# Sorting attention scores from their SBUF copy, whole groups a group ahead, and half of a row sum moved to GpSimd

## The reference, cut to what matters

```
def sparsemax(z):                       # over the 32 patterns
    z_sorted = -sort(-z)
    cum = cumsum(z_sorted)
    support = 1 + k * z_sorted > cum    # k = 1..32
    k_sup = sum(support)
    tau = (cum[k_sup - 1] - 1) / k_sup
    return maximum(z - tau, 0)
...
scores = einsum('blhe,bshe->bhls', queries, keys)
A = sparsemax(scale * scores)
out = einsum('bhls,bshd->blhd', A, values) @ Wo + bo
x = x + layernorm(out)
```

## Time and profile before

| | us |
|---|---|
| median of 3 runs | 487.43 |
| lowest and highest run | 486.13, 487.61 |
| the profiled execution, its time | 487.64 |
| the profiled execution, its span | 485.9 |

### The profile page before, as it was taken

The page is one execution under the profiler, slowest core; times in us unless marked ns, Lnnn a source line. Parts: engine busy times, 40 slices in busy tenths (PEclk is TensorE's granted clock), DMA queues, the critical chain, the costliest instruction groups (busy, mean ns, idle before and its releaser), DMA issues. The chain is left out here.

```text
span 485.9 us, 6975 instructions
## 1 busy us (share of the span) xinstructions
PE 403.1 (83%) x2091; PEld 248.2 (51%) x2091; DVE 310.0 (64%) x1177; ACT 232.1 (48%) x424; POOL 151.9 (31%) x251
## 2 busy tenths in 40 slices
PE   3886566779888987997879999999998679999981
PEld 3542223235444554665646775634443237888870
DVE  3599999969999987586214236233332124979984
ACT  2226647747686795778444734100000001355765
POOL 3105645454858522432201110010000000344453
PEclk9997888788999998999998999999997879999997
DMA  4294011011010229367219667749999999601223
GB/s 145 88 300 127 8 44 43 1 43 38 8 43 2 76 88 309 117 217 275 103 56 316 246 215 262 261 181 395 395 391 396 392 377 368 221 1 45 86 88 129
DMA packets 44030, 83.78 MB, mean 172 GB/s; under 512 B 1878, under 2 KB 36316, under 8 KB 39388
## 3 DMA queue, kind: packets, MB, share of 16 engines
q1 hardware_dynamic: 42936, 82.15, 48.0%
q10 hardware_dynamic: 1060, 1.22, 0.8%
HBM read 70.78 MB, written 12.58 MB: 172 GB/s over the span
## 5 line engine op out<-in xcount | busy, mean ns | idle before, releaser
L1063 PE MATMUL bank<-Wz,yT 128*128 128x512 f32 x128 | 71.0, 707 | 25.9 <-DVE top L1640 23.2
L1063 PEld LDWEIGHTS bank<-Wz,yT 128*128 128x128 f32 x128 | 28.1, 228 | 61.6 <-issue 48.1
L1640 DVE MAX8 top<-bank 128x8 f32<-128x32 f32 x512 | 51.5, 181 | 1.9 <-ACT arena L736 1.7
L997 ACT ACTIVATE d<-d 128x32 f32<-128x32 f32 x16 | 3.7, 229 | 90.6 <-DVE d L2020 90.6
L576 POOL TENSOR_SCALAR veps<-mv 128x4 f32<-128x4 f32 x24 | 6.0, 248 | 107.0 <-DVE mv L1568 75.3
L684 POOL TENSOR_TENSOR work<-work 128x512 f32<-128x512 f32 x16 | 16.6, 1061 | 66.2 <-DVE work L2085 66.2
L1096 PE MATMUL bank<-aWo,hoT 128*128 128x256 f32 x128 | 36.0, 404 | 0.1
L715 ACT ACTIVATE arena<-arena,shift,rstd 128x256 f32<-128x256 f32 x64 | 33.2, 594 | 3.7 <-POOL shift L699 2.9
L1130 PE MATMUL bank<-arena,Wd 128*128 128x512 f32 x64 | 29.2, 598 | 3.2 <-ACT arena L799 3.2
L1159 PE MATMUL bank<-d,work 128*128 128x256 f32 x128 | 30.3, 382 | 0.9 <-ACT d L827 0.9
L1501 PE MATMUL bank<-scr,work 128*128 128x256 f32 x128 | 29.1, 381 | 1.6 <-ACT work L1010 1.6
(11 more groups left out here) (262 smaller groups left out, 879.0 us busy)
## 6 DMA issues: line engine op xcount, KB each, us to landing
arena<-in_L_ffn_e_W_dram SPq DMA_DIRECT2D x10, 1024.0 KB, 7.8
x<-in_L_ffn_e_W_dram SPq DMA_DIRECT2D x9, 1024.0 KB, 9.2
arena<-in_L_ffn_e_Wg_dram SPq DMA_DIRECT2D x7, 1024.0 KB, 11.2
scr<-in_L_ffn_e_W_dram SPq DMA_DIRECT2D x7, 1024.0 KB, 13.7
work<-in_L_ffn_e_W_dram SPq DMA_DIRECT2D x5, 1024.0 KB, 13.7
xin<-in_L_attn_query_dram SPq DMA_DIRECT2D x8, 512.0 KB, 4.1
x<-in_L_attn_query_dram SPq DMA_DIRECT2D x1, 4096.0 KB, 16.6
out_dram<-x SPq DMA_DIRECT2D x8, 512.0 KB, 5.6
```

Source lines behind the costliest of these rows:

```text
L1063: mm = pe.matmul(bZ[t % 2][:, :], yT[:, c, t * P:(t + 1) * P], Wz[:, c, :], start=(c == 0), stop=(c == C - 1))
L1640: mx = v.max(top[:, h * TG + t, :], bZ[t % 2][:, h * NS:(h + 1) * NS])
```

## The change

The sort reads the scores from their copy in SBUF instead of from the bank, so PE only waits until ScalarE has copied a tile (z_sb) and not until DVE has sorted it. In batch 0 the scores of a whole group are made together, a group ahead: PE runs turn_y and four tiles, ScalarE copies four tiles before the signs of the group. DVE sorts all four tiles of group i+1 ahead of the count of group i; threshold comes right behind settle. Group 5's last two tiles, which stood among the heads of batch 0, are made before them. In batch 0 GpSimd adds, behind the roots, the upper 16 of each row of clamped differences to the lower 16 (add_halves, into a free part of arena, semaphore added), and DVE's row sum runs over the 16 results. DVE's loop over groups 1 and 2 is written out. In batch 1 the order of DVE's work stays.

```diff
+        halved = arena[:, 12288:13312]
...
+            def add_halves(i):
+
+                hold(relued, i * 2 + 2)
+                rows_ = d[:, :].rearrange("p (r s) -> p r s", s=NS)
+                pool.tensor_tensor(halved.rearrange("p (r s) -> p r s", s=NS // 2), rows_[:, :, 0:NS // 2],
+                                   rows_[:, :, NS // 2:NS], ALU.add).then_inc(added, 1)
...
             with pool.Fori(0, GB - 1) as i:
                 subtract(i, 0)
                 roots(0, i + 2)
+                add_halves(i)
                 lower(i, 0)
             subtract(GB - 1, 0)
             roots(0, GB + 1)
+            add_halves(GB - 1)
             lower(GB - 1, 0)
...
-            put_scores(1, 0, range(2))
+            put_scores(1, 0, range(TG))
             with act.Fori(0, GB - 2) as i:
                 clamp(i)
                 mark(i)
                 norm_y(i + 2)
-                put_scores(i + 1, 0, range(2, TG))
                 put_yT(i + 2)
-                put_scores(i + 2, 0, range(2))
+                put_scores(i + 2, 0, range(TG))
                 signs(i, 0)
-            clamp(2)
...
+            for i in range(GB - 2, GB):
+                clamp(i)
+                mark(i)
+                norm_y(i + 2)
+                put_yT(i + 2)
+                put_scores(i + 2, 1, range(TG))
+                signs(i, 0)
...
             norm_y(6)
-            put_scores(5, 1, range(2, TG))
             put_yT(6)
...
                     if n >= 2:
-                        pe.wait_ge(topped, n - 1)
+                        pe.wait_ge(z_sb, n - 1)
...
-            scores_of(1, range(2))
+            scores_of(1, range(TG))
             for i in range(GB):
-                scores_of(i + 1, range(2, TG))
                 turn_y(i + 2)
-                scores_of(i + 2, range(2))
+                scores_of(i + 2, range(TG))
...
             heads_of(0, range(3))
-            scores_of(5, range(2, TG))
             turn_y(6)
...
-            def sort_top(i, tiles):
+            def sort_top(i, b, tiles):
 
                 for t in tiles:
                     hold(z_sb, i * TG + (t + 1))
                     for h in range(NH):
-                        mx = v.max(top[:, h * TG + t, :], bZ[t % 2][:, h * NS:(h + 1) * NS])
+                        mx = v.max(top[:, h * TG + t, :],
+                                   scr[b][:, h, bass.ds(i * TG + (t - b * KT), 1), :].rearrange("p o s -> p (o s)"))
                     mx.then_inc(topped, 1)
...
-                v.wait_ge(relued, i * 2 + 2)
-                v.tensor_reduce(exc[:, :], d3, AX_X, ALU.add).then_inc(newton, 1)
+                if b == 0:
+                    hold(added, i + 1)
+                    v.tensor_reduce(exc[:, :], halved.rearrange("p (r s) -> p r s", s=NS // 2), AX_X, ALU.add).then_inc(newton, 1)
+                else:
+                    v.wait_ge(relued, i * 2 + 2)
+                    v.tensor_reduce(exc[:, :], d3, AX_X, ALU.add).then_inc(newton, 1)
...
-            def batch_of_scores(i, b):
+            def batch_of_scores(i, b, nb=0):
 
                 first_statistics(i + 2)
-                sort_top(i + 1, range(2))
+                sort_top(i + 1, nb, range(TG))
                 count(i, b, True)
                 settle(i, b, True)
-                sort_top(i + 1, range(2, TG))
                 threshold(i + 1)
 
             batch_of_scores(0, 0)
-            with v.Fori(1, GB - 1) as i:
+            for i in range(1, GB - 1):
                 batch_of_scores(i, 0)
-            batch_of_scores(GB - 1, 0)
+            batch_of_scores(GB - 1, 0, 1)
```

More of the change, by code:

```diff
@@ L249, in build @@
         diff = sem("diff")
+        added = sem("added")
         relued = sem("relued")
@@ L1908, in _ @@
             own(split3(ab3[:, :], bo3))
-            sort_top(0, range(2))
+            sort_top(0, 0, range(2))
             fold_dispatch()
-            sort_top(0, range(2, TG))
+            sort_top(0, 0, range(2, TG))
             threshold(0)
             keep_dispatch()
-            def batch_of_scores(i, b):
+            def batch_of_scores(i, b, nb=0):
                 first_statistics(i + 2)
-                sort_top(i + 1, range(2))
+                sort_top(i + 1, nb, range(TG))
                 count(i, b, True)
                 settle(i, b, True)
-                sort_top(i + 1, range(2, TG))
                 threshold(i + 1)
             batch_of_scores(0, 0)
-            with v.Fori(1, GB - 1) as i:
+            for i in range(1, GB - 1):
                 batch_of_scores(i, 0)
-            batch_of_scores(GB - 1, 0)
+            batch_of_scores(GB - 1, 0, 1)
             check(0)
@@ L1935, in _ @@
                 v.wait_ge(cum, i * 3 + 3)
-                sort_top(i + 1, range(2))
+                sort_top(i + 1, 1, range(2))
                 if g > 0:
@@ L1942, in _ @@
                 settle(i, 1, False)
-                sort_top(i + 1, range(2, TG))
+                sort_top(i + 1, 1, range(2, TG))
                 threshold(i + 1)
```

## The result

| | before | after |
|---|---|---|
| median | 487.47 us (486.13 to 487.61, 4 runs) | 504.19 us (503.9 to 505.02, 4 runs) |
| ratio after/before | | 1.0349 [1.0327, 1.0371] |
| profiled execution, span | 487.64 us, 485.9 us | 504.1 us, 502.0 us |
| first check (flagi), end of batch 0 | 108.44 | 122.78 |
| second check, end of batch 1 | 190.04 | 203.83 |

The change costs 16.7 us, 3.5%. The forecast was 493.1 with a range up to 496: the sign is right and the size is wrong by 11 us. The profiled executions say where: 14.3 us are lost up to the first check, batch 1 gives back 0.5 (81.05 us from check to check, before 81.60), and 2.3 are lost behind it. The two spans differ by 16.1.

The account below looks back on a forecast made before the run. The prediction took DVE's queue to bound the front part. Longer batch 0 cycles, with DVE blocked by GpSimd's lowering, gave +6.65 us and the end of batch 0 -1.0: +5.65, forecast 493.1 us, range 487 to 496.

Parts of the forecast that it names:

- DVE's queue: Front part of the kernel, both batches: claimed to be as long as DVE's work, busy 66 of 69 us and 75 of 82.
- The end of batch 0: Last signs and flag of batch 0: flag's reduce 2.3 us after the last tau instead of 3.29, giving back 1.0 us.
- T: End of DVE's reduce that makes tau, from which cycles are counted; the last in batch 0 was forecast at 111.80.
- the forecast's better case for DVE: DVE's batch 0 cycle if the scan goes first and the multiply-add waits for GpSimd's lowering: 18.52 us.
- rival 4: Batch 0, later still: bursts stay at the low clock or the addition takes over 2.3 us; 496 to 498, chance 0.05.
- PE's slack: PE waiting for ScalarE's copy instead of the sort: PE is not the bound, so the edit was put at nothing.
- The addition: GpSimd's adding of halves behind the roots in batch 0: taken as 1.91 us, hidden by the sort with no room.
- Rival 1: Batch 0, nothing blocked: the scan passes beside GpSimd's lowering; cycle 16.1 us, -1.9 us, 485.5, chance 0.10.
- rival 2: Batch 0, scan and multiply-add both go ahead of GpSimd's lowering: cycle 17.8 us, +3.6 us, 491.0, chance 0.10.
- Rival 3: The sort, MAX8 cheaper from SBUF: 487 to 490.5, chance 0.08; by the page's full difference about 472, chance 0.02.
- The lock: Batch 0, scan or multiply-add blocked by GpSimd's lowering: cycles of 18.52 or 18.80 us; the blocked forecast had 0.65.
- the middle: Batch 0 cycle taken as 18.66 us, between 18.52 (scan first) and 18.80 (scan blocked).

Follow-up runs that it names:

- e6: After, with tiles made in pairs as in before and nine matmuls without use on PE ahead of the batch 0 transposes: 494.4 us, ratio 1.0143.
- e5: After, with PE running nine matmuls without use between the clamp and the transposes in batch 0: 498.22 us, ratio 1.022.
- e4: Before, with the sort reading SBUF, PE waiting for ScalarE's copy instead of the sort, and DVE's loop written out: 487.85 us, ratio 1.0022.
- e8: Before, with the sort reading SBUF and DVE's loop written out, but PE still waiting for the sort: 486.6 us, ratio 0.9984.
- e1: After, with the multiply-add's second factor read from a copy in PSUM in batch 0: 506.0 us, ratio 1.040.
- e7: After, with tiles in pairs, nine matmuls without use ahead of the transposes, and the multiply-add's factor in PSUM in batch 0: 492.31 us, ratio 1.0093.
- e3: After, with tiles made in pairs as in before and the multiply-add's factor in PSUM in batch 0: 497.41 us, ratio 1.0224.
- e12: Before, with the sort reading SBUF, PE waiting for the sort, and the scan's factors in PSUM in batch 0: 485.59 us, ratio 0.9987.
- e2: After, with before's order on PE and ScalarE, two tiles made ahead of the clamp and two ahead of the signs: 497.45 us, ratio 1.021.

## Why the prediction was wrong

**What bounds the kernel.** Right for before, wrong for after: "DVE's queue" became a round over ScalarE and PE, at 20.3 to 20.7 us for each group, where DVE and GpSimd would allow the 18.8 to 18.9 of e6 (forecast 18.66).

**The step that failed is "The end of batch 0", with the last sentence on steady cycles.** It counted "eight score matmuls", up to 6.59 us. The row with x8 in the earlier trace rows is two tiles: the kernel issues two matmuls for each tile, and the trace has four records for each. So four tiles are sixteen, 8.7 to 9.2 us in after. It also took PE's times from before, where the transposes run at the high level (1.22 us, granted clock 1.00); in after they are 1.98 at 0.50. By that wrong count the signs ended at the latest at T+20.9; in the first cycle of after they end at T+24.6, of which the burst is 2.6 us more than the 6.6 allowed for it and yT 0.8, and in the second at 81.21, T+26.4, well into the next cycle. "In steady cycles the later signs do no harm: the clamp they delay ends before GpSimd's roots do" fell with it: the roots are over at 60.86 and the clamp ends at 62.42. Twice the 6.59 of the earlier trace rows would have been enough to ask the question. With the times of these runs the round reads: 1.99 + 1.91 + 2.06 (ScalarE), transposes 1.2 to 2.0, yT 1.1, sixteen matmuls 7.1 to 8.8, the last copy 0.6, signs 2.1: 18 to 20.5 us without the handings-over between the engines, against the 18.5 of the forecast's better case for DVE. It would have been a rival at the least, with the time of rival 4 or above.

**"PE's slack" as cover was wrong too.** The wait for the sort was read as harmless because it isn't on DVE's path; what PE would do without it, and at which clock, was not asked. e5 and the pair e4, e8 show it: giving PE work shortens the transposes from 1.98 to 1.2 to 1.7 us, and making it wait in pieces to 1.1 to 1.2.

**The addition was mis-sized:** 2.38 us instead of 1.91, above the threshold of 2.3 that rival 4 named. In e6, where nothing else is in the way, it costs 0.65 to 0.8 of waiting in each cycle. Rival 4 (the low clock or a long addition) was the nearest of the rivals, with a chance of 0.05, and too small by 6 us.

**The other rivals.** Rival 1 (nothing blocked) and rival 2 (DVE ahead twice) are out: the multiply-add is blocked in every cycle but the start. Rival 3 needed MAX8 to be 10 to 18 ns cheaper; they are 5 ns cheaper. Where e1 and e7 take the lock away, the first cycle, before the round comes round again, is 15.5 to 15.6, near the 15.8 that rival 1's numbers give for it (49.70 + 2.68 - 36.62).

**What was right.** The lock: scan first, multiply-add 3.95, the lowering 4.53, and a cycle of 18.8 to 18.9 in e6, that is 18.52 and the addition's excess. (The section Who interferes with whom of the page "SBUF — State Buffer" of the Trainium skill, by which whoever issues first holds the pair for the whole instruction, gave that case; the trace agrees, with the multiply-add held and not the scan.) I had taken the middle, 18.66. MAX8 from SBUF: 64 in 6.03, a spacing of (6.03 - 0.18)/63 = 0.093, at the low end of 0.092 to 0.104 and far from the 65 ns less that I had estimated from the page "VectorE: DVE Perf Modes" (section on the TRN2 errata) of the Trainium skill; I had taken no difference for the sum. In e8, where the source differs (and DVE's loop is written out), the first check comes 0.65 us earlier, no more than the scatter of the start, and the second 1.24; part of the gain is lost as the scan grows from 1.56 to 1.73, and what is left can't be told in the median. Batch 1: 81.05 from check to check for a forecast of no change. With the round taken out the forecast's own sum comes out: e6 has its last T at 112.09 (111.80) and the first check at 114.22 (114.1, that is 108.44 + 5.65). That it fits so closely is in part luck: the first cycle is 0.4 us shorter than forecast (18.80 for 19.20), and the three others together are 0.6 longer.

**The forecast left out 2 us behind the second check.** From there to the end it is 295.9 in before, 298.2 in after, 298.0 in e6; in the other kernels between 295.4 (e4) and 298.5 (e7). Ten microseconds near the start of that stretch in before, then in after:

```profile
191.50:201.50 10.00, 9.98 (x58) 6.88 (x56) 6.08 (x22) 8.07 (x17) 3.91 (x10) 0.91 0.54 179
```

```profile
205.00:215.00 10.00, 10.00 (x53) 6.76 (x53) 5.26 (x21) 6.84 (x15) 3.89 (x10) 0.78 0.55 181
```

PE is full in both, and at 0.78 of full speed instead of 0.91 it gets through fewer matmuls (53 for 58). Counted from the check itself, the first ten microseconds are at 0.83 in before and at 0.72 in after and in e6. Why the clock differs there was not tested; it stays open.

## What to carry to other kernels

Before moving a step, write the round that it belongs to across all engines, with the number of instructions of each burst counted from its rows, and compare its length with the cycle of the engine that is full: an order that lengthens the round costs as soon as the two cross. A long wait of an engine that is not the bound may be what spreads its work and keeps its clock up, so ask what the engine does in the time that removing the wait gives it. And test a suspected cost where it is next in line: freeing the same multiply-add gained nothing in the medians of e1 and e3, and some 2 us (not clear of the noise) in e7. Last, check what one count in a row stands for before multiplying it: here x8 was two tiles and not four.

## What the runs showed of the hardware that was not expected

- An addition on GpSimd of 1024 outputs whose inputs are the halves of 32-column rows takes 2.38 us; the subtraction with 1024 outputs takes 1.9. That one reads whole rows of 32 and a tau for each row; which property of the addition makes the difference was not tried.
- Where GpSimd's lowering starts 0.1 us into a scan it takes 4.53 instead of 3.64 us, and the DVE instruction behind the scan (two inputs in SBUF) is then held until it is over: 3.95 instead of 0.69. With one of its inputs in PSUM it takes 0.69 beside the same lowering (e1, e7), and a scan with one input in PSUM 1.22 instead of 1.56 to 1.73 (e12). The lowering stays at 4.54 in e1.
- PE's eight transposes take 1.98 us (granted clock 0.50) after 5 to 9 us without work, and 1.1 to 1.2 (1.00) in before and e8, where it had work less than 1 us before. Nine matmuls without use ahead of them didn't always do: in e5 they take 1.22, 1.42, 1.23 and 1.71, and in the first cycle of e7 again 1.98. Sixteen score matmuls take 7.03 us at a granted clock of 1.00 (at the start of these kernels) to 10.21 at 0.69 (e2).
